# Adjacency product with a fused layer norm on one core: x moved to a third transfer queue, adj issued quadrant by quadrant

## Chip, core and metric

One core of one Trainium2 chip. The metric is the device time of one launch in microseconds; the kernel before takes 1008.75 us in the median of three runs (1007.6 to 1009.8). Lower is better.

## What is computed

```python
# x: (8192, 256) f32, adj: (8192, 8192) f32, weight: (256, 256) f32
bw = sign(weight)
ba = maximum(sign(x), 0)
xw = ba @ bw.T
out = layernorm(x + relu(adj @ xw), axis=-1)      # eps 1e-5
```

The product with adj is nearly all of the work: adj has 268 MB, x 8.4 MB, and each element of adj is read once.

## The kernel before

The 8192 rows of the result are made in 16 blocks of 512 (`NBLK`, `MB`). In a block the contraction runs over 8192 rows of xw, in 8 chunks of 1024 (`CH`, `KC`), a chunk in 4 units (`UPC`), so a block has 32 units (`UB`) and the kernel 512 (`UNITS`). Chunks are numbered through all blocks, 128 in all. adj has to be turned so that the contraction lies on the partitions. A chunk (2.1 MB) is loaded in four quadrants of 32 partitions (512 KB, rows of 1 KB) into one of four slots of `raw`, and VectorE turns it in 32x32 blocks, one unit (128x1024) at a time (`turn`, line 362), into SBUF (units of kind P) or PSUM (kind V; 10 of 32). ScalarE copies a unit as `hi`, rounded to the matmul's type (`make_hi`, line 263). The rest, `lo`, is the turned unit less `hi`: GpSimd makes it for kind P (line 243), VectorE for kind V (line 366). TensorE multiplies a unit in 8 matmuls, `hi` and `lo` each against xw (`use_unit`, line 490). The ring of hi and lo has 6 units (`RING`), and four turned units of kind P may wait.

xw is made during block 0, in 16 groups of 512 rows (two groups for each chunk): VectorE compares x with 0 (`make_step`, line 340), TensorE turns the result (`turn_step`, line 465) and multiplies it with the signs of the weight (`make_xw`, line 475), and ScalarE copies both out of PSUM (lines 252 and 256). After unit n with n even TensorE makes group n/2 + 1 and turns group n/2 + 2. VectorE compares the two groups of chunk c after it has turned the last unit of chunk c-1.

x is loaded in nine pieces (`X_PIECES`): 0 and 1 are half a chunk's worth (512 KB in all), pieces 2 to 8 hold 1024 rows each (1 MB in four quadrants of 256 KB), piece c+1 for chunk c. `LOWER` is quadrants 0 and 1 (partitions 0 to 63), `UPPER` 2 and 3. SP issues the lower quadrants of x and adj, ScalarE's queue (ACT) the upper ones, between its own instructions. SP also loads 512 rows of x for the end of each block (`load_rows`) and stores the result (`store_rows`). Chunk 0 comes as two halves (`start_half`).

When a transfer is issued is written out by hand. For chunk s, `issue_at[s]` is the unit after whose copy ACT issues the first upper quadrant; the second follows one unit later. For s = 2 to 7 it is 2, 6, 10, 14, 18, 22, for 8 to 12 it is 25, 28, 31, 34, 37, then 4(s-3). SP issues both lower quadrants at once, for chunks 2 to 12 when ScalarE has copied that unit (`his_made`), and it never issues before the slot's former chunk is turned (`units_turned`). Pieces 3 to 8 of x are issued at units `x_at` = 0, 3, 7, 11, 15, 19, by both queues, on SP ahead of the chunk. Piece 2 is issued at the start.

After its last unit a block is rectified by ScalarE (line 272), turned back by TensorE (line 515) and normalised, beside the next block's units.

Of the kernel before, what the change touches and what calls it, by code (L numbers as in the profile page):

```python
# [6 lines left out]
G = P // Q  # L7
# [3 lines left out]
def build(nc, x, adj, w, out):  # L11
# [9 lines left out]
    SLOTS = 4  # L21
    CH = 8
# [3 lines left out]
    NCHUNK = NBLK * CH  # L26
    UK = 2
    UE = UK * MB
    UPC = KB // UK
# [22 lines left out]
    def ordinal(n):  # L52
        return before[kinds[n]][n]
# [14 lines left out]
    with ctx:  # L68
# [3 lines left out]
        def sem(name):  # L72
            return ctx.enter_context(nc.semaphore(name))
# [56 lines left out]
        units_turned = sem("units_turned")  # L130
        his_made = sem("his_made")
# [18 lines left out]
        LOWER, UPPER = range(0, G // 2), range(G // 2, G)  # L150
# [4 lines left out]
        def start_chunk(eng, ch, quadrants):  # L155
            for g in quadrants:
                eng.dma_start(raw_view(ch)[g * Q:(g + 1) * Q],
                              adj_v[ch // CH, ch % CH, g]).then_inc(adj_loaded[ch % SLOTS], 16)
# [8 lines left out]
        def start_x(eng, i, quadrants):  # L167
            first, count = X_PIECES[i]
            c, k = first // KB, first % KB
            for g in quadrants:  # L170
                eng.dma_start(x_sb[g * Q:(g + 1) * Q, first:first + count],  # L171
                              x_turn[c, g, :, k:k + count]).then_inc(x_loaded[i], 16)

        issue_at = [max(UPC * (s - SLOTS + 1) + (0 if s > CH + 4 else CH + 5 - s if s >= CH else 6), 0)
                    for s in range(NCHUNK)]
        x_at = [max(UPC * c - 9, 0) for c in range(CH)]

        @block.sync  # L180
        def _(sp):
            sp.dma_start(w_sb, w_rows).then_inc(w_loaded, 16)
            for i in range(2):
                start_x(sp, i, LOWER)
                start_half(sp, i, LOWER)

            def load_chunk(ch):
                if ch >= SLOTS:

                    sp.wait_ge(units_turned, (ch - SLOTS + 1) * UPC)  # L190
                if 2 <= ch <= CH + 4:
                    sp.wait_ge(his_made, issue_at[ch] + 1)
                start_chunk(sp, ch, LOWER)

            def store_rows(b):
                sp.wait_ge(blocks_done, b + 1)
                sp.dma_start(out_rows[b], rows[:]).then_inc(rows_stored, 16)

            def load_rows(b):
                if b == 0:  # L200

                    sp.wait_ge(xw_made, GROUPS)
                else:
                    sp.wait_ge(rows_stored, b * 16)
                sp.dma_start(rows[:], x_rows[b]).then_inc(rows_loaded, 16)

            for c in range(1, CH):
                if c >= 2:
                    sp.wait_ge(his_made, x_at[c] + 1)
                start_x(sp, c + 1, LOWER)  # L210
                load_chunk(c)
            for b in range(1, NBLK):
                for c in range(CH):
                    load_chunk(b * CH + c)
                    if c == 2 and b >= 2:
                        store_rows(b - 2)
                    if c == 3:
                        load_rows(b - 1)
            store_rows(NBLK - 2)
            load_rows(NBLK - 1)  # L220
            for b, ms in PIECES:
                if b == NBLK - 1:
                    sp.wait_ge(blocks_done, NBLK)
                else:
                    sp.wait_ge(last_piece_done, 1)
                sp.dma_start(out_rows[NBLK - 1, :, ms[0]:ms[-1] + 1],
                             rows[:, ms[0]:ms[-1] + 1]).then_inc(rows_stored, 16)
            sp.wait_ge(rows_stored, (NBLK - 1 + len(PIECES)) * 16)

        @block.gpsimd  # L230
        def _(pool):
            pool.memset(eps[:], EPS).then_inc(eps_set, 1)
            pool.memset(ident[:], 0.0).then_inc(zeroed, 1)
            pool.memset(ident_b[:], 0.0).then_inc(zeroed, 1)
            pool.wait_ge(zeroed, 2)
            for m in (ident, ident_b):
                pool.affine_select(out=m[:], in_=m[:], compare_op=ALU.not_equal, fill=1.0, base=0,
                                   pattern=[[-1, P]], channel_multiplier=1).then_inc(idents_made, 1)
            for n in range(UNITS):
                if kinds[n] == "P":  # L240

                    pool.wait_ge(his_made, n + 1)
                    pool.tensor_tensor(lo[:, n % RING], turned[:, ordinal(n) % TP], hi[:, n % RING].bitcast(f32),  # L243
                                       ALU.subtract).then_inc(p_los_made, 1)

        @block.scalar
        def _(act):
            def copy_step(n):
                act.wait_ge(steps_turned, n + 1)
                if n >= 2:  # L250
                    act.wait_ge(xw_made, n - 1)
                act.activation(step_xT[:, n % 2], ps_xT[n % 2], ACT.Copy).then_inc(steps_copied, 1)  # L252

            def copy_xw(n):
                act.wait_ge(xw_made, n + 1)
                act.activation(xw[:, n * GK:(n + 1) * GK], ps_xw, ACT.Copy).then_inc(xw_copied, 1)  # L256

            def make_hi(n):
                act.wait_ge(units_turned, n + 1)
                if n >= RING:  # L260
                    act.wait_ge(units_used, n - RING + 1)
                src = turned[:, ordinal(n) % TP] if kinds[n] == "P" else turned_v
                act.activation(hi[:, n % RING], src, ACT.Copy).then_inc(his_made, 1)  # L263

            def make_relu(b):
                act.wait_ge(first_halves, b + 1)
                if b:
                    act.wait_ge(relus_turned, b * MT)
                for a in range(DH):
                    if a == 1:  # L270
                        act.wait_ge(units_used, (b + 1) * UB)
                    act.activation(relu[:, a], acc[b % 2][a], ACT.Relu).then_inc(relus_made, 1)  # L272

            def make_std(n, ms):
                act.wait_ge(mvs_made, n + 1)
                act.activation(std[:, ms], mv[:, ms, 1], ACT.Sqrt, bias=eps[:]).then_inc(stds_made, 1)

            def normalise(n, m, last):
                act.wait_ge(shifts_made, n + 1)
                done = act.activation(rows[:, m], rows[:, m], ACT.Identity,  # L280
                                      bias=shift[:, m:m + 1], scale=rstd[:, m:m + 1])
                if last:
                    done.then_inc(blocks_done, 1)

            def ending(b, u):
                if u == RING - 1:
                    make_relu(b)
                if u == 18:
                    make_std(b, slice(0, MT))
                if 22 <= u < 22 + MT:  # L290
                    normalise(b, u - 22, u - 22 == MT - 1)

            act.wait_ge(eps_set, 1)
            act.activation(warm[:], eps[:], ACT.Copy)
            for i in range(2):
                start_x(act, i, UPPER)
                start_half(act, i, UPPER)
            start_x(act, 2, UPPER)
            start_chunk(act, 1, UPPER)
            for n in range(UNITS):  # L300
                make_hi(n)
                if n == 0:
                    copy_step(1)
                for c in range(2, CH):
                    if n == x_at[c]:
                        start_x(act, c + 1, UPPER)
                for s in range(2, NCHUNK):

                    if n == issue_at[s]:
                        start_chunk(act, s, UPPER[0:1])  # L310
                    if n == issue_at[s] + 1:
                        start_chunk(act, s, UPPER[1:2])
                if n < UB:
                    g = n // UPG
                    if n % UPG and g >= 1:
                        copy_xw(g)
                    if n % UPG and 1 <= g < GROUPS - 1:
                        copy_step(g + 1)
                else:
                    ending(n // UB - 1, n % UB)  # L320
            make_relu(NBLK - 1)
            for n, ms in PIECES:
                make_std(n, slice(ms[0], ms[-1] + 1))
            n, ms = PIECES[0]
            for m in ms:
                normalise(n, m, m == ms[-1])
# [234 lines left out]
```

## Time and profile before

| | |
|---|---|
| median of three runs | 1008.75 us |
| the profiled execution | 1006.04 us |
| its span, first to last instruction | 1004.1 us |
| TensorE busy | 975.0 us, 97% |
| VectorE busy | 857.1 us, 85% |
| GpSimd busy | 842.1 us, 84% |
| ScalarE busy | 613.2 us, 61% |
| bytes moved | 294.67 MB, mean 293 GB/s |
| queue q1 | 155.47 MB |
| queue q10 | 138.43 MB |

The page gives the busy time of each engine and a chain of waits, which goes back from the last instruction to what released it at each step. Times in the views are microseconds from the start of the span. In the tables by windows and by queue, a queue's share is the time of its packets as a share of 16 transfer engines, and can be over 100%. A row of a timeline may join neighbouring instructions of one line (x2, x16), with their time together.

### The profile page before, as it was taken

The numbers are of one execution on the slowest core, as the hardware profiler recorded it, in microseconds if no ns is written. First come the engines' busy times: TensorE is split into PE (matmuls) and PEld (weight loads), VectorE is DVE, ScalarE is ACT, GpSimd is POOL, SyncE is SP. The second block draws the span as 40 slices with busy tenths as digits, with TensorE's granted clock in tenths as the row PEclk, the third lists the DMA queues.
The fourth block names the chain that finished last, engine by engine and source line by source line (L and its number), as shares of the span: only waits on it lengthen the run. The fifth ranks groups of instructions, "written<-read, shape, count | busy, mean of one in ns | idle before, by whom it ended". The sixth has DMA issues, their size and how long they took to land.

```text
span 1004.1 us, 12250 instructions
## 1 busy us (share of the span) xinstructions
PE 975.0 (97%) x4484; PEld 803.2 (80%) x4484; DVE 857.1 (85%) x873; ACT 613.2 (61%) x656; POOL 842.1 (84%) x361
## 2 busy tenths in 40 slices
PE   5798999999999999999999999999999999999996
PEld 3686888888888888888888888888888888888885
DVE  6859799998889898888988889898988989898893
ACT  3666767565656656566665657566565665656662
POOL 3455889898989988898998889989888998889893
PEclk9999999999999999999999999999999999999998
DMA  9999999999999999999999999999999999999961
GB/s 283 315 236 279 289 336 338 298 339 298 301 309 300 315 293 321 297 287 313 294 322 289 312 300 291 299 317 312 290 310 296 303 310 301 324 283 308 305 186 42
DMA packets 298459, 294.67 MB, mean 293 GB/s; under 512 B 9376, under 2 KB 298400, under 8 KB 298400
## 3 DMA queue, kind: packets, MB, share of 16 engines
q1 hardware_dynamic: 157792, 155.47, 57.1%
q10 hardware_dynamic: 140608, 138.43, 49.7%
q8 instruction: 35, 0.57, 0.3%
q14 instruction: 24, 0.20, 0.1%
HBM read 285.47 MB, written 8.39 MB: 293 GB/s over the span
## 4 chain that ended last, share of the span: by engine, by line
PE 91%; DMA 4%; DVE 2%; ACT 1%; issue 1%; SPq 0%; ACTq 0%; DVEq 0%
PE ps L490 89%; DMA raw<-in_adj_dram 4%; PE ps L515 1%; DVE turned L362 1%; DVE relu L340 1%; PE ps L475 0%; ACT hi L263 0%; PE ps L465 0%; ACT rows L252 0%; DVE lo L366 0%; SPq L171 0%; DVE stats L374 0%; ACTq L171 0%; SPq L164 0%; DVE rows L370 0%
## 5 line engine op out<-in xcount | busy, mean ns | idle before, releaser
L243 POOL TENSOR_TENSOR lo<-turned,hi 128x1024 fp32r<-128x1024 f32 x352 | 841.0, 2411 | 145.2 <-ACT hi L263 141.2
L490 PE MATMUL ps<-hi,xw 128*128 128x512 f32 x2048 | 802.4, 392 | 4.7 <-DVE lo L366 2.6
L490 PE MATMUL ps<-lo,xw 128*128 128x512 f32 x2048 | 799.3, 390 | 0.0
L263 ACT ACTIVATE hi<-turned 128x1024 fp32r<-128x1024 f32 x352 | 373.5, 1062 | 263.3 <-PE ps L490 166.5
L490 PEld LDWEIGHTS ps<-hi,xw 128*128 128x128 f32 x2048 | 385.5, 188 | 86.3 <-ACT xw L256 4.0
L490 PEld LDWEIGHTS ps<-lo,xw 128*128 128x128 f32 x2048 | 385.7, 188 | 79.3
L362 DVE STREAM_TRANSPOSE turned<-raw 128x1024 f32<-128x1024 f32 x352 | 426.3, 1218 | 5.0 <-DMA raw<-in_adj_dram 5.0
L366 DVE TENSOR_TENSOR lo<-ps,hi 128x1024 fp32r<-128x1024 f32 x160 | 195.1, 1220 | 104.5 <-ACT hi L263 104.5
L263 ACT ACTIVATE hi<-ps 128x1024 fp32r<-128x1024 f32 x160 | 164.0, 1025 | 91.1 <-PE ps L490 74.1
L362 DVE STREAM_TRANSPOSE ps<-raw 128x1024 f32<-128x1024 f32 x160 | 195.2, 1220 | 10.5 <-DMA raw<-in_adj_dram 10.5
L280 ACT ACTIVATE rows<-rows,shift,rstd 128x256 f32<-128x256 f32 x62 | 36.2, 586 | 0.0
L370 DVE TENSOR_TENSOR rows<-ps,rows 128x1024 f32<-128x1024 f32 (+1 forms) x17 | 19.4, 1141 | 14.2 <-PE ps L515 12.2
L340 DVE TENSOR_SCALAR relu<-x_sb 128x1024 bf16<-128x1024 f32 x16 | 23.2, 1478 | 1.6 <-DMA x_sb<-in_x_dram 1.0
L256 ACT ACTIVATE xw<-ps 128x1024 fp32r<-128x1024 f32 x15 | 15.3, 1021 | 14.2 <-PE ps L475 10.5
L272 ACT ACTIVATE relu<-ps 128x512 f32<-128x512 f32 x32 | 17.2, 585 | 9.2 <-PE ps L490 9.2
L374 DVE BATCH_NORM_STATS2 stats<-rows 128x6 f32<-128x256 f32 x64 | 22.4, 412 | 0.1
L465 PE MATMUL ps<-ident_b,relu 128*128 128x128 bf16 x128 | 10.6, 231 | 9.5 <-DVE relu L340 9.5
L475 PE MATMUL ps<-sign_wT,rows 128*128 128x256 bf16 x128 | 18.5, 292 | 0.9 <-DVE rows L413 0.9
L252 ACT ACTIVATE rows<-ps 128x1024 bf16<-128x1024 bf16 x15 | 15.3, 1018 | 5.3 <-PE ps L465 5.3
L465 PEld LDWEIGHTS ps<-ident_b,relu 128*128 128x128 bf16 x128 | 8.7, 103 | 11.6 <-DVE relu L340 11.3
L475 PEld LDWEIGHTS ps<-sign_wT,rows 128*128 128x128 bf16 x128 | 12.0, 104 | 7.0 <-issue 5.3
L515 PE MATMUL ps<-ident,relu 128*128 128x128 f32 x128 | 16.8, 273 | 0.2 <-ACT relu L272 0.2
(25 smaller groups left out, 47.8 us busy)
## 6 DMA issues: line engine op xcount, KB each, us to landing
raw<-in_adj_dram ACTq DMA_DIRECT2D x254, 512.0 KB, 12.0
raw<-in_adj_dram SPq DMA_DIRECT2D x254, 512.0 KB, 11.2
rows<-in_x_dram SPq DMA_DIRECT2D x16, 512.0 KB, 10.3
out_dram<-rows SPq DMA_DIRECT2D x15, 512.0 KB, 15.9
x_sb<-in_x_dram ACTq DMA_DIRECT2D x14, 256.0 KB, 11.5
x_sb<-in_x_dram SPq DMA_DIRECT2D x14, 256.0 KB, 13.8
raw<-in_adj_dram ACTq DMA_DIRECT2D x4, 256.0 KB, 8.3
raw<-in_adj_dram SPq DMA_DIRECT2D x4, 256.0 KB, 8.9
```

The lines of the kernel that those rows point to most:

```text
L243: pool.tensor_tensor(lo[:, n % RING], turned[:, ordinal(n) % TP], hi[:, n % RING].bitcast(f32), ALU.subtract).then_inc(p_los_made, 1)
L263: act.activation(hi[:, n % RING], src, ACT.Copy).then_inc(his_made, 1)
L280: done = act.activation(rows[:, m], rows[:, m], ACT.Identity, bias=shift[:, m:m + 1], scale=rstd[:, m:m + 1])
L340: dve.tensor_scalar(step_x[:, n % STEP_BUFS], x_sb[:, n * GK:(n + 1) * GK], 0.0, None, ALU.is_gt).then_inc(steps_made, 1)
L362: dve.transpose(dst.rearrange("p (k t j) -> p k t j", k=UK, j=Q), src).then_inc(units_turned, 1)
L366: dve.tensor_tensor(lo[:, n % RING], turned_v[:, :], hi[:, n % RING].bitcast(f32), ALU.subtract).then_inc(v_los_made, 1)
L370: dve.tensor_tensor(rows[:, ms], back[:, ms], rows[:, ms], ALU.add).then_inc(sums_made, 1)
L374: dve.bn_stats(stats[:, m], rows[:, m]).then_inc(stats_made, 1)
L465: last = pe.transpose(ps_xT[n % 2][:, k, i], step_x[:, n % STEP_BUFS, k, i * P:(i + 1) * P], ident_b[:])
L475: last = pe.matmul(ps_xw[:, k], step_xT[:, n % 2, k, i], sign_wT[:, i], start=(i == 0), stop=(i == DH - 1))
L490: return pe.matmul(acc[b % 2][a], xw[:, step, a * P:(a + 1) * P], part[:, n % RING, k * MB:(k + 1) * MB], start=(step == 0 and part is hi) ...
L515: last = pe.transpose(back[:, m, a * P:(a + 1) * P], relu[:, a, m * P:(m + 1) * P], ident[:])
```

## The change

GpSimd issues pieces 2 to 8 of x, four quadrants at a time: piece 2 right after it has made the identity matrices, piece c+1 when unit max(4c - 10, 0) is turned (units 0, 2, 6, 10, 14, 18 for c = 2 to 7), between its subtractions. SP and ACT keep pieces 0 and 1 of x, and adj. Chunks 2 to 7 are now issued one quadrant by each of the two at unit 4(c-2), and one at 4(c-2)+2; ACT issues after its copy of that unit, SP when VectorE has turned it. For chunks 8 to 12 ACT's units are 23, 26, 29, 32, 36 and the one after each; SP issues both quadrants as soon as the slot is free. From chunk 13 on nothing changes.

```diff
-        issue_at = [max(UPC * (s - SLOTS + 1) + (0 if s > CH + 4 else CH + 5 - s if s >= CH else 6), 0)
-                    for s in range(NCHUNK)]
-        x_at = [max(UPC * c - 9, 0) for c in range(CH)]
+        def issue_at(ch, half):
+            early = 4 + 2 * half if ch < CH else max(CH + 3 - ch, 0) + half
+            return max(UPC * (ch - SLOTS + 1) + early, 0)
+
+        def x_at(c):
+            return max(UPC * c - 10, 0)
...
-                if 2 <= ch <= CH + 4:
-                    sp.wait_ge(his_made, issue_at[ch] + 1)
                 start_chunk(sp, ch, LOWER)
...
-            for c in range(1, CH):
-                if c >= 2:
-                    sp.wait_ge(his_made, x_at[c] + 1)
-                start_x(sp, c + 1, LOWER)
-                load_chunk(c)
+            load_chunk(1)
+            for c in range(2, CH):
+
+                for half in range(2):
+                    sp.wait_ge(units_turned, issue_at(c, half) + 1)
+                    start_chunk(sp, c, LOWER[half:half + 1])
...
+            start_x(pool, 2, range(G))
             for n in range(UNITS):
+                for c in range(2, CH):
+                    if n == x_at(c):
+
+                        pool.wait_ge(units_turned, n + 1)
+                        start_x(pool, c + 1, range(G))
                 if kinds[n] == "P":
...
-            start_x(act, 2, UPPER)
             start_chunk(act, 1, UPPER)
             for n in range(UNITS):
                 make_hi(n)
                 if n == 0:
                     copy_step(1)
-                for c in range(2, CH):
-                    if n == x_at[c]:
-                        start_x(act, c + 1, UPPER)
-                for s in range(2, NCHUNK):
-
-                    if n == issue_at[s]:
-                        start_chunk(act, s, UPPER[0:1])
-                    if n == issue_at[s] + 1:
-                        start_chunk(act, s, UPPER[1:2])
+                for ch in range(2, NCHUNK):
+
+                    for half in range(2):
+                        if n == issue_at(ch, half):
+                            start_chunk(act, ch, UPPER[half:half + 1])
```

## Rows read from the trace of the kernel before

**Rows 1.** The page: busy us, share, instructions; queue: packets, MB, share.
```profile
PE 975.0 (97%) x4484; PEld 803.2 (80%) x4484; DVE 857.1 (85%) x873; ACT 613.2 (61%) x656; POOL 842.1 (84%) x361
...
q1 hardware_dynamic: 157792, 155.47, 57.1%
```
**Rows 2.** Chain of waits in order of time: start us, us, what.
```profile
20.23 16.84 DMA raw<-in_adj_dram
...
68.68 14.97 DMA raw<-in_adj_dram
...
92.18 2.74 DVE relu L340
...
94.97 0.62 PE ps L465 x8
...
100.19 0.45 PE ps L465 x8
...
104.36 0.89 PE ps L475 x8
105.25 14.56 PE ps L490 x64
...
120.68 58.05 PE ps L490 x256
...
994.81 0.61 ACT relu L272
```
**Rows 3.** Table by windows: stretch, length, busy us, clock, DMA share, GB/s.
```profile
0.00:15.00 15.00, 4.52 (x28) 2.94 (x28) 7.28 (x10) 2.85 (x4) 1.12 (x9) 1.00 0.99 241
15.00:43.00 28.00, 24.12 (x130) 17.95 (x131) 23.70 (x17) 16.82 (x18) 15.79 (x7) 1.00 1.10 346
44.50:50.50 6.00, 3.24 (x23) 2.52 (x22) 6.00 (x5) 3.29 (x4) 2.34 (x1) 0.90 1.13 213
53.00:58.00 5.00, 5.00 (x33) 4.07 (x32) 2.97 (x4) 2.74 (x3) 0.65 (x1) 1.00 1.15 219
45.00:105.00 60.00, 53.47 (x326) 42.36 (x325) 45.67 (x39) 39.38 (x41) 32.71 (x14) 0.97 1.12 256
```
**Rows 4.** Queues from 44.5 to 50.5 us, then 53 to 58: packets, MB, share.
```profile
q10 hardware_dynamic: 1190, 1.17, 104.1%
q1 hardware_dynamic: 117, 0.10, 9.3%
...
q1 hardware_dynamic: 1041, 1.02, 107.6%
q10 hardware_dynamic: 64, 0.06, 5.4%
```
**Rows 5.** Timelines of ACT's and SP's queues: start us, us, instruction.
```profile
41.78 0.32 ACTq L157 DMA_DIRECT2D raw<-in_adj_dram  x1
...
55.79 0.32 ACTq L157 DMA_DIRECT2D raw<-in_adj_dram  x1
...
44.52 0.84 SPq L157 DMA_DIRECT2D raw<-in_adj_dram  x2
```
**Rows 6.** Timeline of VectorE: first units of chunks 1, 5 and 6.
```profile
25.23 1.26 DVE L362 STREAM_TRANSPOSE ps<-raw 128x1024 f32<-128x1024 f32 x1 [0.49 <-DMA raw<-in_adj_dram]
...
73.53 1.26 DVE L362 STREAM_TRANSPOSE ps<-raw 128x1024 f32<-128x1024 f32 x1 [5.66 <-DMA raw<-in_adj_dram]
...
83.67 1.25 DVE L362 STREAM_TRANSPOSE turned<-raw 128x1024 f32<-128x1024 f32 x1 [0.84 <-DMA raw<-in_adj_dram]
```
**Rows 7.** Timeline, all engines: copy of unit 5, first matmul of unit 4.
```profile
27.63 1.06 ACT L263 ACTIVATE hi<-turned 128x1024 fp32r<-128x1024 f32 x1
...
29.66 0.50 PE L490 MATMUL ps<-hi,xw 128*128 128x512 f32 x1
```
**Rows 8.** GpSimd: group of 0 to 112 us; timeline, units 18 and 19.
```profile
L243 POOL TENSOR_TENSOR lo<-turned,hi 128x1024 fp32r<-128x1024 f32 x24 | 57.5, 2409 | 53.8 <-ACT hi L263 53.7
...
68.33 4.73 POOL L243 TENSOR_TENSOR lo<-turned,hi 128x1024 fp32r<-128x1024 f32 x2 [1.77 <-ACT hi L263]
```

## The prediction

> **What bounds the kernel now.** The page's busy line is read first: TensorE works 975.0 of 1004.1 us [rows 1], so only some 29 us can be won at all. The chain of waits in order of time says where. From 94.97 us on it holds TensorE alone until 994.81, in blocks of 58.05 us for 32 units [rows 2]. Whatever transfers, GpSimd or VectorE do after 95 us is covered. The time is set by how early TensorE ends its last stall. I measure that by one event, the start of unit 29, at 105.25 us [rows 2]. A gain there comes off the end one for one.
>
> Before it, the chain's long links are transfers of adj: 16.84 us up to 37.07 and 14.97 us up to 83.65 [rows 2]. So in block 0 the transfers set the pace. The table by windows shows that it isn't their total rate. From 15 to 43 us the core moves 346 GB/s, from 45 to 105 us only 256, with stretches at 213 and 219 [rows 3]. The queue table of two of these stretches shows why: from 44.5 to 50.5 us queue q10 moved 1.17 MB and q1 0.10; from 53 to 58 us q1 moved 1.02 and q10 0.06 [rows 4]. q1 is SP: its 155.47 MB in the whole run [rows 1] are half of adj (134.2 MB) and of x (4.2), and rows and out (16.8), which SP alone moves. One queue alone gives about 205 to 215 GB/s, both together 346. ACT issues four transfers (two of adj, two of x) from 41.78 us on, SP its four from 44.52 on, and ACT next at 55.79 [rows 5]. Yet SP's bytes hardly flow before ACT's are through. Batches of one half of the partitions go one after the other, at some 60% of the rate.
>
> **What the change does to the transfers.** (a) Fourteen transfers of x leave ACT's queue and fourteen SP's (pieces 2 to 8, two quadrants each). (b) SP and ACT each issue one quadrant of adj per unit, at units 4(c-2) and 4(c-2)+2 for chunk c of block 0. Before, it was two units later, and SP's wait was on ScalarE's copy. SP's wait is now for VectorE's turn; behind it on SP lie only further loads. (c) GpSimd issues pieces of 1 MB.
>
> Supply per chunk is 2.1 MB of adj and 1.05 of x, 3.15 MB. At 256 GB/s that is 12.3 us (rows 3), which the first units of chunks 1, 5 and 6 confirm roughly: 25.23, 73.53, 83.67 [rows 6], 11.7 us a chunk. With an equal share of three queues, two of them always on the same half while x flows, the doubled half gets its 205 and the other half as much as one queue: 308 GB/s, 10.2 us a chunk. If x doesn't hinder, it is 346 and 9.1 us. These two are my bounds for the supply.
>
> At the start the change costs. Piece 2 now flows beside the first pieces, and piece 3 is issued at the first turned unit, beside chunk 1. Up to 15 us the core moves 241 GB/s, 3.6 MB [rows 3]. Of the 5.5 MB in SP's and ACT's queues up to the end of chunk 1 (w, pieces 0 and 1, the two halves of chunk 0, chunk 1) 2.55 are then through instead of nearly all 3.6, as 1.05 are piece 2. The other 2.95 at two thirds of 308 or of 346 GB/s take 14.4 or 12.8 us: chunk 1 is there at 27.8 to 29.4, and with a latency of some 1 us I take 29.5, against 25.23 [rows 6]: 4.3 us late. From there chunk 6 comes five periods later, at 75.0 (9.1 us) to 80.5 (10.2 us), against 83.67. From 83.67 to unit 29 it is 21.6 us in the trace; so by the supply unit 29 starts at 96.6 to 102.1, a gain of 3.2 to 8.6 us.
>
> **TensorE's own pace.** A unit costs 58.05/32 = 1.81 us, a group of xw 0.89 and its turn 0.45 [rows 2]; a chunk of block 0 has four units and two groups, 9.94 us. Unit 4 can't start before about 29.5 + 4.4 = 33.9. The 4.4 is what lies in the trace between the turn of unit 4 at 25.23 [rows 6] and its start on TensorE at 29.66 [rows 7]. From there 25 units, 13 groups and 12 turns are 62.3 us: unit 29 at 96.2, a gain of 9.0. This is a ceiling.
>
> **What GpSimd pays.** The trace has no transfer issued by GpSimd, so its price T stays open. Each makes GpSimd's work wait, as its instructions run in order; 28 are added. Below it lies what an unhindered issue costs ScalarE, 0.32 us [rows 5]; nothing excludes that it is partly hidden, but not below zero. Above it I put GpSimd's own subtraction, 2.41 us [rows 8]. The middles of 0.32 and 2.41 are 0.88 (geometric) and 1.37; each transfer has 256 rows to be described, so it isn't near the low end. I take T = 1.1. The wait for a turned unit that is added ahead of each piece holds nothing up: behind it lies the subtraction of the same or a later unit, which needs that unit anyway. The exception is the first piece, which nothing waits behind.
>
> GpSimd has 24 subtractions up to 112 us, 57.5 us busy and some 54 idle [rows 8]. That idle time covers the new work only in part, since it lies in the stalls that are to go. Per chunk it is 2.75 x 2.41 + 4T = 6.6 + 4T, at T = 1.1 11.0 us, more than TensorE's 9.94. Unit 5 is the first of GpSimd's in chunk 1; in the trace its copy, begun at 27.63 [rows 7], ends 3.5 us after the turn of unit 4 begins, so it starts at 33.0. Up to unit 19 GpSimd has eleven subtractions and four pieces: 26.5 + 16T, end at 59.5 + 16T. In the trace that end is 73.06 [rows 8]. From it TensorE needs ten units, five groups and four turns, 24.4 us: unit 29 at 83.9 + 16T. At T = 1.1 that is 101.5; at 0.32 89.0 (then supply and TensorE bind); at 2.41 122.5. Break-even with 105.25 is T = 1.33.
>
> **A rule against it.** In this case's trace two queues with one half of the partitions each move 346 GB/s together, 213 when one is alone [rows 3, 4]. The Trainium skill, SBUF — State Buffer, "Can I just issue two DMAs to hit both halves?", says that they serialize, with only 6% gained. By that, pairing the quadrants would bring nothing; the trace disagrees. Its page DMA: Bandwidth & Descriptors, Issuing engines are not separate DMA queues, says that more issuing engines save the sequencer's time alone; no row here has a third queue, and that is rival C.
>
> **What else is touched.** ACT loses two issues of 0.4 us in each chunk, which shortens the copies' wait; I count it as part of the coupling. VectorE's comparison of x takes 2.74 us in the chain [rows 2], beside a GpSimd at work; with GpSimd fuller this may grow by as much as one such wait, and I let the two cancel. Chunks 8 to 12 are issued two units earlier; in block 1 TensorE never waits, so I cost this at nothing. If block 1 were starved, each chunk late would cost its lateness.
>
> **The sum.** The latest of TensorE 96.2, supply 96.6 to 102.1 (middle 99.4), GpSimd 101.5: unit 29 at 101.5, GpSimd next to supply. The gain is 3.75 us. The profiled execution took 1006.04 us, with 1004.1 of span and 1.9 around it; the median is 1008.75, 2.7 above. I take the gain off the median: 1005.0.
>
> **Rivals.**
> A, the forecast: 1005.0, own range 1001.5 to 1006.7 (T from 0.9 to 1.2).
> B, GpSimd's issues are cheap (T under 0.8) and x doesn't hinder (346 GB/s): unit 29 at 96.6, time 1000.1. For it: both queues at 346 GB/s from 15 to 43 us with x among them. Against: there x was on the same two queues, halves matched.
> C, the third queue brings no bandwidth: transfers are served about in the order of issue, as SP's batch from 44.52 on suggests, so x in front of adj costs what it cost before, or T lies between 1.2 and 1.45. Time 1008.75.
> D, slower: GpSimd becomes the bound of block 0. The place is units 5 to 19, the price 16 transfers at T - 1.33 each, and it decides from T = 1.46 (2 us late). At T = 1.8, unit 29 at 112.7, 7.4 us late: 1016.2; at 2.41 it would be 1026. For it: 6.6 us of subtractions per chunk leave only 3.3 us for four issues.
>
> **Chances.** A 0.37, B 0.10, C 0.21, D 0.32. A gain or loss of 0.2%, 2 us, is about what can be told from no change. A's upper end overlaps that by little: faster 0.46, same 0.22, slower 0.32. The range goes from 999.0 (a bit under B) to 1018.0 (D up to T = 1.9), leaving about 0.15 out above and below.
>
> **What would show it.** Right: a third queue with some 7.3 MB, both adj queues active together in every window from 45 to 85 us, 300 GB/s or more there, GpSimd near 100% busy between 30 and 75 us, unit 4's turn at about 29.5, unit 29's start near 101.5, the chain without long adj links. Wrong: rates still at 210 in stretches (C); GpSimd's transfers at over 1.46 us each, with TensorE waiting for GpSimd's lo in chunks 2 to 4 (D); TensorE idle after 110 us.

## The result and the profile after

The changed kernel takes 1014.21 us (six runs, 1013.75 to 1016.27) against 1008.17 us for the kernel before, measured beside it: a ratio of 1.0064, 95% interval 1.0048 to 1.0080. It is 6 us slower, where the prediction had 1005.0 and a gain. The profiled execution took 1014.44 us, of which 1012.6 are span. It is 8.4 us above the profiled execution of the kernel before (1006.04), where the medians are 6.0 apart, so the times of events below are those of one execution each.

The page of the changed kernel: busy time, the queues (packets, MB, share), and the group of GpSimd's transfers (busy, mean ns | idle before).

```profile
PE 976.4 (96%) x4484; PEld 805.2 (80%) x4484; DVE 849.9 (84%) x873; ACT 612.6 (60%) x656; POOL 859.0 (85%) x389
...
DMA packets 293083, 294.67 MB, mean 291 GB/s; under 512 B 9376, under 2 KB 291232, under 8 KB 293024
...
q1 hardware_dynamic: 153984, 151.80, 55.8%
q10 hardware_dynamic: 136800, 134.76, 48.1%
q0 software_dynamic: 2240, 7.34, 3.0%
...
L171 POOL DMA_DIRECT2D x_sb<-in_x_dram x28 | 17.5, 630 | 12.9 <-DVE ps L365 12.8
```

TensorE does the same work [rows 1], so the span grew by waiting. Two numbers matter at once. A transfer costs GpSimd 0.63 us, cheap. And the third queue, q0, moved its 7.34 MB in 2240 packets, 3277 bytes each on average, where the other two move about 985 bytes per packet (151.80 MB in 153984). The packet line shows the same: 1792 packets lie between 2 and 8 KB (293024 less 291232), and 7.34 MB in 1792 packets is 4 KB each, four rows of x. The rest of q0's packets are tiny. A packet of SP's or ACT's holds one row of 1 KB.

The chain of waits of the changed kernel, in order of time (start us, us, what):

```profile
5.32 7.07 SPq L157
...
12.44 24.11 DMA raw<-in_adj_dram
36.55 0.02 issue
36.57 1.26 DVE ps L365
...
40.99 3.78 PE ps L493 x8
44.77 1.65 PE ps L478 x8
...
55.52 3.83 DVE relu L343
...
60.05 5.30 PE ps L493 x16
...
66.69 3.71 PE ps L493 x16
...
76.91 15.20 DMA raw<-in_adj_dram
...
100.65 2.75 DVE relu L343
...
103.45 0.62 PE ps L468 x8
...
113.73 14.56 PE ps L493 x64
...
129.17 58.08 PE ps L493 x256
```

Unit 29 starts at 113.73, against 105.25 [rows 2], 8.48 us later, and the span is 8.5 us longer. After it TensorE alone follows, at the same 58.05 to 58.08 us for 32 units. So all of the loss lies in block 0, as the prediction had placed it. A quadrant of chunk 1 was issued at 12.44 us, after SP had been held 7.07 us in the issue of the one before, and landed 24.11 us later. Unit 4 is turned at 36.57, against 25.23 [rows 6]. From there to unit 24, turned at 92.13, it is 55.6 us, against 58.4 before: the start is lost (11.3 us), and a little of it won back.

The table by windows of the changed kernel (stretch, length, busy us of PE, PEld, DVE, ACT, POOL, clock, transfer share, GB/s):

```profile
0.00:15.00 15.00, 3.49 (x20) 2.14 (x20) 4.06 (x6) 1.49 (x2) 3.58 (x13) 1.00 0.96 217
15.00:43.00 28.00, 16.21 (x77) 12.06 (x78) 14.23 (x15) 12.10 (x13) 15.01 (x13) 0.87 1.10 284
45.00:105.00 60.00, 55.31 (x341) 44.49 (x339) 42.26 (x37) 40.43 (x42) 42.83 (x27) 0.96 1.09 282
91.00:107.00 16.00, 14.19 (x91) 11.47 (x90) 13.24 (x11) 11.46 (x12) 8.61 (x5) 1.00 1.10 347
```

Against [rows 3] the rate fell from 241 to 217 and from 346 to 284 GB/s in the first two stretches, and rose from 256 to 282 in the third. Once x is through, at 91 us, it is 347. TensorE's granted share of its clock in the second stretch is 0.87: it was at 1.2 GHz for part of it, around a stall of 7.1 us that ended at 41 us.

This lower clock is on the chain too. At 40.99 us 8 matmuls took 3.78 us and the group of xw behind them 1.65 (granted clock 0.52 from 41 to 46.4 us), and at 60.05 us 16 matmuls took 5.30 (0.69 from 60 to 65.3 us); at the full clock 16 matmuls take 3.71 and a group 0.89. Together the chain is 4.3 us longer by it (1.9, 0.8 and 1.6). The chain of the kernel before has one such place:

```profile
49.01 5.32 PE ps L490 x16
```

That is 1.6 us, so some 2.7 us of the 8.48 are the clock. In both kernels it was low right after TensorE had stalled; in e1_adj_alone below it is 1.00 from 15 to 105 us. Another 1.1 us is VectorE's comparison of x, 3.83 us at 55.52, where the chain before has 2.75 us.

What q0 does to the others shows in the queues from 23 to 27 us, when chunk 1 and piece 3 flow (packets, MB, share):

```profile
q0 software_dynamic: 203, 0.64, 63.1%
q10 hardware_dynamic: 201, 0.20, 22.5%
q1 hardware_dynamic: 202, 0.19, 21.9%
```

The three queues get the same number of packets, 203, 201 and 202. GpSimd's are over three times as large, so x takes 62% of the bytes (0.64 of 1.03 MB), and the two queues of adj share 0.39 MB in 4 us, 98 GB/s, where [rows 3] had 346 for adj and x together. In sum it is 259 GB/s. Why the sum falls from 347 isn't shown. A reading that fits: one quadrant of x lands on one half of the partitions, and that half, at 164 GB/s of x plus 48 of adj, carries about the 205 to 215 GB/s which one queue alone reaches in [rows 3, 4], while the other half gets only the packets that its turns give it, 48 GB/s. But no run tells the two halves apart. What the rows do show is that a packet of adj takes longer beside x, in both queues alike: some 70 ns (21.9% of 16 engines in 4 us, over 202 packets), against 50 where SP and ACT flow evenly (e1_adj_alone below) and 84 with one queue alone [rows 4]. The Trainium skill, DMA: Bandwidth & Descriptors, Queues, rings and completion order, says that a transfer engine takes turns between the queues packet by packet; with that the trace agrees, to 1% in these 4 us.

The turns explain the loss where all three queues have work. Later in block 0 adj's queues are often empty while x flows. From 70 to 74 us:

```profile
q0 software_dynamic: 234, 0.77, 93.7%
q10 hardware_dynamic: 38, 0.04, 5.0%
q1 hardware_dynamic: 34, 0.03, 4.5%
```

With work in them, adj's queues would have had as many packets as q0. They had next to nothing ready, though ACT had issued a quadrant at 67.12 us, and the rate is 213 GB/s.

### The profile page after: what moved, and what is told of

Its sections match the earlier page's. It is cut to its first block, busy times and chain, and to the rows that moved or that the text cites. A ratio compares the mean times of both kernels' runs of the same rounds, so it can differ in the third digit from the quotient of the medians.

```text
span 1012.6 us, 12241 instructions
## 1 busy us (share of the span) xinstructions
PE 976.4 (96%) x4484; PEld 805.2 (80%) x4484; DVE 849.9 (84%) x873; ACT 612.6 (60%) x656; POOL 859.0 (85%) x389
## 2 busy tenths in 40 slices
DMA packets 293083, 294.67 MB, mean 291 GB/s; under 512 B 9376, under 2 KB 291232, under 8 KB 293024
## 3 DMA queue, kind: packets, MB, share of 16 engines
q1 hardware_dynamic: 153984, 151.80, 55.8%
q0 software_dynamic: 2240, 7.34, 3.0%
## 4 chain that ended last, share of the span: by engine, by line
PE 92%; DMA 4%; DVE 2%; SPq 1%; ACT 1%; issue 1%; ACTq 0%; DVEq 0%
PE ps L493 89%; DMA raw<-in_adj_dram 4%; PE ps L518 1%; SPq L157 1%; PE ps L478 1%; DVE relu L343 1%; DVE turned L365 0%; PE ps L468 0%; ACT hi L271 0%; SPq L171 0%; SPq L164 0%; ACT rows L260 0%; DVE stats L377 0%; ACT xw L264 0%; DVE rows L373 0%
## 5 line engine op out<-in xcount | busy, mean ns | idle before, releaser
L171 POOL DMA_DIRECT2D x_sb<-in_x_dram x28 | 17.5, 630 | 12.9 <-DVE ps L365 12.8
## 6 DMA issues: line engine op xcount, KB each, us to landing
raw<-in_adj_dram SPq DMA_DIRECT2D x254, 512.0 KB, 11.3
```

## Experiments

The theories: P, the queues take turns by packets, so x starves adj (above). S, the new times of adj cost by themselves. G, GpSimd's own time, 17.5 us, costs. H, the order of GpSimd's quadrants, costs. Each run was compared with the kernel before on the same chip; ratios are to it, with 95% intervals. e7_half_rows was run once, for its trace. A direct test of P, with packets of adj as large as those of x, was not run.

### One part at a time

**e1_adj_alone**: the new times of adj, x left on SP and ACT.

```diff
-            return max(UPC * c - 10, 0)
+            return max(UPC * c - 9, 0)
...
+            start_x(sp, 2, LOWER)
             load_chunk(1)
-            for c in range(2, CH):
-                for half in range(2):
-                    sp.wait_ge(units_turned, issue_at(c, half) + 1)
-                    start_chunk(sp, c, LOWER[half:half + 1])
+            for n in range(UB):
+                for c in range(2, CH):
+                    if n == x_at(c):
+                        sp.wait_ge(his_made, n + 1)
+                        start_x(sp, c + 1, LOWER)
+                for c in range(2, CH):
+                    for half in range(2):
+                        if n == issue_at(c, half):
+                            sp.wait_ge(units_turned, n + 1)
+                            start_chunk(sp, c, LOWER[half:half + 1])
...
-            start_x(pool, 2, range(G))
             for n in range(UNITS):
-                for c in range(2, CH):
-                    if n == x_at(c):
-
-                        pool.wait_ge(units_turned, n + 1)
-                        start_x(pool, c + 1, range(G))
...
+            start_x(act, 2, UPPER)
             start_chunk(act, 1, UPPER)
...
+                for c in range(2, CH):
+                    if n == x_at(c):
+                        start_x(act, c + 1, UPPER)
```

> The changed kernel's schedule of adj, with x left on SP and ACT at the units of the kernel before (SP: piece 2 ahead of chunk 1, then each piece at its unit, ahead of adj of the same unit). Theory P (packets): GpSimd's queue takes turns with the other two packet by packet, its packets are over 3 KB against 1 KB, so x takes two thirds of the rate and adj starves; without that queue the loss is gone: 1003 to 1009 us. Theory S (schedule): the new times of adj cost by themselves, 1012 to 1015 us. Theory G (GpSimd's own time, 28 x 0.63 us = 17.5 us): as P, at most 1009.

Measured: 1000.51 us, ratio 0.9924 (0.9908 to 0.9941). Faster than expected, and faster than both kernels by some 7.5 and 14 us. S is dead. From the changed kernel this run differs in who issues x and also, by up to one unit, in when. The windows show where its gain over the kernel before comes from:

```profile
15.00:43.00 28.00, 24.91 (x136) 19.27 (x136) 20.46 (x17) 18.35 (x20) 17.79 (x7) 1.00 1.10 347
45.00:105.00 60.00, 56.25 (x344) 45.66 (x345) 44.94 (x41) 41.84 (x44) 36.88 (x16) 1.00 1.11 307
```

The late stretch runs at 307 GB/s, against 256 [rows 3]. In the very window in which q10 had been alone [rows 4], 44.5 to 50.5 us, both queues now flow evenly:

```profile
q1 hardware_dynamic: 1048, 1.04, 55.3%
q10 hardware_dynamic: 1049, 1.04, 54.5%
```

**e2_x_alone**: the other part, pieces 2 to 8 on GpSimd, adj at its old times.

```diff
-        x_at = [max(UPC * c - 9, 0) for c in range(CH)]
+        x_at = [max(UPC * c - 10, 0) for c in range(CH)]
...
             for c in range(1, CH):
-                if c >= 2:
-                    sp.wait_ge(his_made, x_at[c] + 1)
-                start_x(sp, c + 1, LOWER)
                 load_chunk(c)
...
+            start_x(pool, 2, range(G))
             for n in range(UNITS):
+                for c in range(2, CH):
+                    if n == x_at[c]:
+                        pool.wait_ge(units_turned, n + 1)
+                        start_x(pool, c + 1, range(G))
...
-            start_x(act, 2, UPPER)
             start_chunk(act, 1, UPPER)
...
-                for c in range(2, CH):
-                    if n == x_at[c]:
-                        start_x(act, c + 1, UPPER)
```

> The kernel before with one part of the change: pieces 2 to 8 of x issued by GpSimd at the changed kernel's units, adj at the old times. P: at least as slow as the changed kernel, as adj is issued later still and meets the same queue: 1013 to 1020 us, with the rate of adj at about 100 GB/s while x flows. S: 1008 us. G: 1012 to 1015 us.

Measured: 1024.17 us, ratio 1.0157 (1.0133 to 1.0181). In P's direction and beyond its band (1013 to 1020), and more than G allowed. So the change is the sum of a part that wins 0.8% and one that costs; beside the new times the third queue costs 1.4% (0.9924 to 1.0064), beside the old ones 1.6%.

### How the third queue costs

**e7_half_rows**: the changed kernel, with chunk 1 of adj loaded in rows of 512 bytes.

```diff
             for g in quadrants:
+                if ch == 1:
+                    for i, done in enumerate((chunk1_half, adj_loaded[1])):
+                        k0, k1 = i * KG // 2, (i + 1) * KG // 2
+                        eng.dma_start(raw_view(1)[g * Q:(g + 1) * Q, :, k0:k1],
+                                      adj_v[0, 1, g, :, :, k0:k1]).then_inc(done, 16)
+                else:
...
+                    if ch == 1:
+                        dve.wait_ge(chunk1_half, G * 16)
```

> The changed kernel with chunk 1 of adj loaded in rows of 512 bytes in place of 1 KB (two transfers for each quadrant), beside pieces 3 and 4 of x. It measures the rule of turns. If a queue's share goes by its packets' size (P), GpSimd's share beside chunk 1 rises from 63% of 260 GB/s (164 against 48 for each other queue, 3.4 to 1) to about 6 or 7 to 1, some 28 GB/s for each of the others, and chunk 1 lands 5 to 15 us later. If shares go by something else (a priority, bytes), the ratio stays near 3.4.

The queues from 23 to 27 us:

```profile
q0 software_dynamic: 229, 0.74, 78.2%
q10 hardware_dynamic: 229, 0.11, 15.7%
q1 hardware_dynamic: 225, 0.11, 15.4%
```

Again equal packets, 229, 229 and 225, now with 0.11 MB for each queue of adj, about 28 GB/s. The ratio went from 3.3 to 6.7 (0.74 to 0.11), as turns by packets demand and no fixed share does. The second half of the expectation missed: unit 4 was turned at 37.53, only 1 us later, since the third queue is empty from 28 to 29 us and again from 35 us on, and adj then flows at 279 to 318 GB/s. The single time, 1015.52 us, says no more than that little changed.

**e4_quadrant_order**: GpSimd's quadrants in the order 0, 2, 1, 3.

```diff
-            start_x(pool, 2, range(G))
+            start_x(pool, 2, (0, 2, 1, 3))
...
-                        start_x(pool, c + 1, range(G))
+                        start_x(pool, c + 1, (0, 2, 1, 3))
```

> The changed kernel with GpSimd's four quadrants issued in the order 0, 2, 1, 3 instead of 0, 1, 2, 3, so that its queue changes between the lower and upper half of the partitions with each transfer. Theory H (halves): two lower quadrants in a row burden the half on which SP's adj lands; with the order changed the rate beside x rises from about 257 to over 290 GB/s and the time falls to 1005 to 1010 us. P: at each moment one quadrant of x flows beside both of adj, whatever the order: rate and time stay, 257 GB/s and 1013 to 1015 us.

Measured: 1013.69 us, ratio 1.0055 (1.0040 to 1.0070), and the rate from 23 to 27 us is 256 GB/s, against 259:

```profile
23.00:27.00 4.00, 3.96 (x26) 2.67 (x24) 1.81 (x3) 3.53 (x4) 3.99 (x6) 1.00 1.07 256
```

H is dead, in time and in rate.

**e6_filler**: the kernel before, with memsets on GpSimd in place of transfers.

```diff
+            fills = 0
             for n in range(UNITS):
+                for c in range(2, CH):
+                    if n == max(UPC * c - 10, 0):
+                        pool.wait_ge(units_turned, n + 1)
+                        for _ in range(10):
+                            if fills:
+                                pool.wait_ge(filled, fills)
+                            pool.memset(fill[:], 0.0).then_inc(filled, 1)
+                            fills += 1
```

> The kernel before, with no transfer on GpSimd, but with ten memsets one after the other (some 2.5 us together) where the changed kernel has GpSimd issue pieces 3 to 8. It measures GpSimd's time alone. G: most of the loss, 1012 to 1015 us. P: GpSimd is idle for 54 us in block 0, its 15 us are covered: 1007 to 1010 us.

Measured: 1006.6 us, ratio 0.9989 (0.9973 to 1.0004): no change, and just below P's band. The fillers took 3.0 to 3.4 us each time, 20 us in all, more than the 17.5 of the transfers.

**e12_adj_alone_filler**: the same with eight memsets, in e1_adj_alone, where transfers hold things up less.

```diff
+            fills = 0
             for n in range(UNITS):
+                for c in range(2, CH):
+                    if n == max(UPC * c - 10, 0):
+                        pool.wait_ge(units_turned, n + 1)
+                        for _ in range(8):
+                            if fills:
+                                pool.wait_ge(filled, fills)
+                            pool.memset(fill[:], 0.0).then_inc(filled, 1)
+                            fills += 1
```

> e1_adj_alone with eight memsets one after the other on GpSimd (some 2.7 us) at each of the six places where the changed kernel has it issue pieces 3 to 8. It prices GpSimd's own time where the transfers are no longer in the way. The changed kernel is 13.7 us slower than e1_adj_alone; theory P gives nearly all of that to the transfers of x and little to GpSimd's time: 1000 to 1003 us here. Theory G: 1006 us or more.

Measured: 998.91 us, ratio 0.9920 (0.9903 to 0.9937), just below P's band and not to be told from e1_adj_alone. A line of its timeline of GpSimd (start us, us):

```profile
31.20 2.90 POOL L257 MEMSET fill<- 128x128 bf16 x8
```

G is dead at both paces: this much of GpSimd's time costs nothing here. A memset isn't a transfer, though. Whether issuing a transfer holds up other engines is read from the traces: VectorE's 16 comparisons of x took 1.01 us each on average in the changed kernel, 1.48 in the kernel before, though one on the chain, at 55.52, was 1.1 us longer. TensorE waited 0.4 us in all for a subtraction on GpSimd.

### Where in block 0 it costs

**e3_piece2_back**: the changed kernel, piece 2 on SP and ACT again.

```diff
+            start_x(sp, 2, LOWER)
             load_chunk(1)
...
-            start_x(pool, 2, range(G))
...
+            start_x(act, 2, UPPER)
             start_chunk(act, 1, UPPER)
```

> The changed kernel with piece 2 of x back on SP and ACT, behind the first pieces and ahead of chunk 1, all else as changed. P: the first half of chunk 0 lands near 11 us instead of 15.7, some 4 us are won at the start, of which pieces 3 and 4 ahead of chunk 1 take back a part: 1010 to 1012 us. G: GpSimd was idle at the time of piece 2, so no change, 1014 us. S: 1014 us.

Measured: 1012.36 us, ratio 1.0044 (1.0030 to 1.0058), just above P's band and 0.2% less than the change, with intervals that overlap. The first unit is turned at 11.85 us again, but chunk 1 isn't there before 35 us:

```profile
35.23 1.26 DVE L366 STREAM_TRANSPOSE ps<-raw 128x1024 f32<-128x1024 f32 x1 [7.91 <-DMA raw<-in_adj_dram]
```

**e8_x_behind_chunk1**: as e3_piece2_back, with pieces 3 and 4 issued at unit 4.

```diff
-            return max(UPC * c - 10, 0)
+            return max(UPC * c - 10, 4)
```

> As e3_piece2_back, and pieces 3 and 4 are issued by GpSimd at unit 4, when chunk 1 has landed, instead of at units 0 and 2. P: chunk 1's first unit is turned near 25 us instead of 35, and TensorE's two stalls of 5.7 and 3.5 us before 40 us go; piece 3 then lands near 34 us, where its comparison is due at 31, which takes 3 us back, and later pieces cost what they cost: 1004 to 1009 us. If the place of these pieces doesn't matter: 1012 us.

Measured: 1009.52 us, ratio 1.0015 (1.0004 to 1.0027), just above P's band. It is faster than e3_piece2_back, with intervals apart, so the place of pieces 3 and 4 matters. The trace shows the trade:

```profile
25.44 1.26 DVE L366 STREAM_TRANSPOSE ps<-raw 128x1024 f32<-128x1024 f32 x1 [0.72 <-DMA raw<-in_adj_dram]
...
40.59 1.29 DVE L344 TENSOR_SCALAR relu<-x_sb 128x1024 bf16<-128x1024 f32 x2 [9.28 <-DMA x_sb<-in_x_dram]
```

Chunk 1 is turned at 25.44, as in [rows 6], but now x is late: its comparison waits 9.28 us for piece 3, to 40.59. I had put piece 3 at 34 us. GpSimd issued it and piece 4 from 27.02 us on:

```profile
27.02 4.77 POOL L171 DMA_DIRECT2D x_sb<-in_x_dram  x8 [2.84 <-DVE ps L366]
```

Its queue has no packet before 32 us, 5 us after the issue, and then needs 6.4 us for a piece at 164 GB/s and the time until the last of it has landed.

**e5_one_quadrant_per_unit**: as e3_piece2_back, GpSimd's quadrants one per unit.

```diff
-                    if n == x_at(c):
-                        pool.wait_ge(units_turned, n + 1)
-                        start_x(pool, c + 1, range(G))
+                    for g in range(G):
+                        if n == x_at(c) + g:
+                            pool.wait_ge(units_turned, n + 1)
+                            start_x(pool, c + 1, range(g, g + 1))
```

> Piece 2 of x back on SP and ACT (as in e3_piece2_back), and GpSimd issues the later pieces one quadrant per unit, from the same first unit on, instead of four at a time. If the loss is one of bursts, adj flows between them and the time falls to 1003 to 1008 us. If it is the share and the rate while x flows (theory P, 257 GB/s in place of 347 for each of some 38 us), it hardly matters how the 38 us are spread: 1008 to 1013 us.

Measured: 1011.15 us, ratio 1.0031 (1.0015 to 1.0046), within P's band, and not clearly under e3_piece2_back. Spreading the bursts doesn't cure it.

### What in the new times of adj wins

**e10_paired_old_times**: the kernel before, SP's lower quadrants one per unit at ACT's units.

```diff
-                load_chunk(c)
+                if c == 1:
+                    load_chunk(c)
+                else:
+                    for half in range(2):
+                        sp.wait_ge(his_made, issue_at[c] + half + 1)
+                        start_chunk(sp, c, LOWER[half:half + 1])
```

> The kernel before, with SP issuing the lower quadrants of chunks 2 to 7 one per unit, at the units at which ACT issues the upper ones, and no other edit: the pairing without the earlier times. If the 7.4 us of e1_adj_alone come from the pairing (both halves of the partitions under way at once), most of it shows here: 1001 to 1004 us. If they come from the earlier issue (no queue runs dry), the single-queue stretches of 205 to 215 GB/s remain: 1006 to 1009 us.

Measured: 1007.11 us, ratio 1.0004 (0.9989 to 1.0018): no change. Its late stretch is that of [rows 3], 255 GB/s against 256:

```profile
45.00:105.00 60.00, 53.43 (x326) 42.36 (x324) 45.71 (x39) 39.42 (x41) 32.58 (x14) 0.97 1.12 255
```

But the edit did less than its expectation says. SP's queue in this run:

```profile
44.50 1.25 SPq L157 DMA_DIRECT2D raw<-in_adj_dram  x2
...
45.44 0.31 SPq L157 DMA_DIRECT2D raw<-in_adj_dram  x1
```

SP waits for ScalarE's copy, so its two quadrants still leave late and nearly together, at 44.50 and 45.44 us. In the kernel before it was 44.52 and 44.87, and ACT's two left at 41.78 and 43.74. A real pairing of the two queues at the old times was not run.

**e11_early_bursts**: e1_adj_alone, both quadrants of a chunk at its first unit, 4(c-2).

```diff
-            early = 4 + 2 * half if ch < CH else max(CH + 3 - ch, 0) + half
+            early = 4 if ch < CH else max(CH + 3 - ch, 0) + half
```

> e1_adj_alone with both quadrants of a chunk issued at its first unit 4(c-2), on SP and on ACT: the earlier times without one quadrant per unit. If the earlier issue is what counts, 999 to 1002 us; if the spacing by unit is, 1004 to 1008 us.

Measured: 1002.49 us, ratio 0.9953 (0.9936 to 0.9970), just above the band of the earlier issue, with the late stretch at 297 GB/s:

```profile
45.00:105.00 60.00, 55.80 (x337) 44.97 (x336) 43.44 (x39) 41.69 (x43) 35.36 (x15) 0.97 1.11 297
```

So the earlier issue gives about 0.5%. The spacing by unit perhaps gives the rest; the intervals of e11 and e1 just overlap, and e10 hardly spaced the issues, so that part stays open.

**e9_piece3_later**: e1_adj_alone, piece 3 at unit 1.

```diff
-            return max(UPC * c - 9, 0)
+            return max(UPC * c - 9, 1)
```

> e1_adj_alone with piece 3 of x at unit 1 instead of 0 on both queues. In e1_adj_alone the copies of units 1 to 3 on ScalarE come 1 to 1.5 us later than before, since ACT's issues at unit 0 are held up, and TensorE stalls 2.1 us at 24 us. If that stall is worth its length, 998 to 1000 us; if a later stall takes its place, 1000.5 us.

Measured: 1001.03 us, ratio 0.9941 (0.9925 to 0.9956): no gain. The stall at 24 us gives way to another, as its second case said.

## Why the prediction was wrong, step by step

**What bounds the kernel: right.** The end is set in block 0, by the transfers. Unit 29's start moved by 8.48 us and the span by 8.5.

**Why the rate was low: half right.** The stretches at 205 to 215 GB/s were one queue alone, and with both flowing it is 347. But the prediction blamed batches of one half of the partitions. Issuing earlier, still in batches, lifted the rate from 256 to 297 (e11). The queues ran dry because they were refilled too late: SP's batch was issued from 44.52 us on, and from 49 to 50 us SP's queue still sent no packet, from 51 to 52 us 131. Why it takes 6 us from issue to flow stays open. The split of SP's batch in e10 (1.0004) was too small to speak for or against batches.

**The supply: the step that failed.** "With an equal share of three queues" I had x at a third and 308 GB/s in sum. The shares are equal in packets, not in bytes: x takes 62%, adj is left 98 GB/s where I gave it 205, and the sum is 259, below the lower of my two bounds for the supply. As an estimate, 7.34 MB at 164 GB/s keep the third queue active for 45 us. If in each of them 88 GB/s are lost to 347, that is 3.9 MB, or 11 us of transfer, of the same size as the 14 us (1.4%) which the queue costs beside the new times. The match is rough: in the later pieces adj's queues were partly empty, and the lower clock adds its own 2.7 us. Order matters too: x that isn't due yet goes ahead of adj that is (e8_x_behind_chunk1).

**The start: right in kind, mis-sized.** The prediction had chunk 1 4.3 us late, at 29.5. It was 11.3 us late, at 36.57, by the same step. SP was also held 7.07 us in one issue (the chain of the changed kernel), which I hadn't counted, and the sum had no term for TensorE's clock after a stall.

**GpSimd's price: too high.** I took T = 1.1 us, and with it GpSimd as the bound. T is 0.63 us, and e6 and e12 show that 20 and 16 us of other work there cost nothing. Rival D ends on the right side, but its mechanism isn't there: by its formula, unit 29 would have started at 83.9 + 16 x 0.63 = 94.0. TensorE waited 0.4 us in all for a subtraction on GpSimd up to 112 us. The slower outcome was given 0.32, for a reason that the runs refute.

**The rival that was missing.** A third queue can be worse than none. Rival C took as its worst that it brings nothing. The measured 1014.21 lies inside the range to 1018.0 only because D had stretched it.

**What was costed at nothing: right.** Chunks 8 to 12 issued earlier: TensorE has no wait after unit 28 in either kernel. ACT without its issues of x: not separable here. The text is off in a detail: for chunks 2 to 7 ACT's first quadrant goes two units earlier, the second only one, and chunk 12 goes one unit earlier.

**The signs.** The third queue moved its 7.34 MB as said. Of the signs that the forecast was right, the others failed: 262 GB/s from 45 to 85 us in place of 300, adj's queues almost empty from 70 to 74 us, GpSimd 60% busy from 30 to 75 us. The signs of C and D were rates at 210 in stretches (213 from 70 to 74 us) and transfers above 1.46 us each (they were 0.63).

**The rule that spoke against it.** The Trainium skill's rule that further issuing engines save only the time of issuing (DMA: Bandwidth & Descriptors, Issuing engines are not separate DMA queues) points the right way, and the cost, 1.4% to 1.6%, is even beyond it. The other, that two transfers to the two halves serialize (SBUF — State Buffer, "Can I just issue two DMAs to hit both halves?"), is contradicted again: in e1_adj_alone two queues, each with its half, hold 347 GB/s from 15 to 43 us, against 213 with one alone [rows 3].

## What to carry to other kernels

Before a transfer moves to a further queue, compare the packet sizes of the queues that will be active together: the turns here are per packet, so the queue with the large packets takes the bytes, whether they are due or not. When a change has two parts, price them apart; here the new issue times alone win 0.8% (1000.51 us), and the third queue hides that win and 0.6% more. Where a rate falls to that of one queue, first see whether the other was refilled in time. And read from the trace whether an edit moved what it was to move: e10 shifted one issue by half a microsecond.

## What was unexpected of the hardware

Three queues with work got equal numbers of packets to 2% (203, 201, 202; with rows of 512 bytes 229, 229, 225). A transfer issued by GpSimd, with 256 rows of 1 KB, goes in packets of 4 KB, four rows each, and some tiny ones (3.3 KB on average), those of SP and ACT in one packet per row. It costs GpSimd 0.63 us, and its first packet comes some 5 us after the issue (issued at 17.29 us, none before 22; in e8_x_behind_chunk1 at 27.02, none before 32). SP's queue in the kernel before was as slow beside a full queue of ACT's (issued from 44.52 us on, no packet from 49 to 50). Beside transfers of GpSimd the rate of all queues together falls from 347 to 259 GB/s, and with rows of 512 bytes to 241.
